# One unrolled plan for everything in front of the layers of a two-part transformer kernel

## The reference

```python
x = x + _layernorm(_L0_attn_ref(_layernorm(x), ...))
# inside, D = 128, H = 16 heads of 8, NB = 32 clusters a head, MLP = 512
x = _layernorm(inputs, ln1_g, ln1_b)
q = einsum('bsd,dhf->bshf', x, Wq); k, v likewise
qb = softmax(einsum('bshf,hfn->bshn', q, Whq)); kb likewise of k and Whk
logits = einsum('bqhf,bkhf->bhqk', q, k) / sqrt(8)
logits = logits + 0.1 * einsum('bqhn,bkhn->bhqk', qb, kb)
out = einsum('bhqk,bkhf->bqhf', softmax(logits), v)
x = einsum('bqhf,hfd->bqd', out, Wo) + inputs
y = _layernorm(x, ln2_g, ln2_b)
y = relu(y @ W1 + b1) @ W2 + b2
return x + y
```

## Time and profile before

| what | us |
| --- | --- |
| median of 3 runs | 3577.6 (3573.7 to 3582.4) |
| the profiled execution | 3577.4 |
| its span in the trace | 3575.6 |
| PE busy | 3290.2 (92%) |
| DVE busy | 2679.8 (75%) |
| ACT busy | 1740.4 (49%) |
| POOL busy | 1999.6 (56%) |

### The profile page before, as it was taken

How to read it: one execution, slowest core, us unless ns; L and a number is a source line. 1 busy time by engine, 2 the same in 40 slices (tenths; PEclk the granted TensorE clock), 3 DMA queues, 4 the chain that set the end, 5 groups by cost and what they waited for, 6 DMA issues and landing times. The chain is left out here.

```text
span 3575.6 us, 54667 instructions
## 1 busy us (share of the span) xinstructions
PE 3290.2 (92%) x17992; PEld 2168.8 (61%) x17992; DVE 2679.8 (75%) x4395; ACT 1740.4 (49%) x3293; POOL 1999.6 (56%) x1584
## 2 busy tenths in 40 slices
PE   5899989957999999999999999999999999999997
PEld 2455555435666666766666676666666766666676
DVE  7877877456787876778787677778786788878666
ACT  3276657633433446553434474443446654343464
POOL 2100000014777767676877656787867667787764
PEclk9588988977999999999999999999999999999999
DMA  0000000024223314632323154332324533232143
GB/s 16 0 2 2 1 1 1 1 62 103 57 63 72 72 25 148 174 82 60 72 63 71 43 173 131 72 72 66 69 48 123 162 98 70 59 72 63 34 157 117
DMA packets 139610, 248.15 MB, mean 69 GB/s; under 512 B 28416, under 2 KB 55936, under 8 KB 139072
## 3 DMA queue, kind: packets, MB, share of 16 engines
q1 hardware_dynamic: 139328, 244.64, 26.4%
HBM read 82.17 MB, written 27.53 MB: 31 GB/s over the span
## 5 line engine op out<-in xcount | busy, mean ns | idle before, releaser
L1128 ACT ACTIVATE prob<-psA 128x512 f32<-128x512 f32 x1152 | 652.7, 596 | 1048.1 <-PE psA L1440 459.2
L971 POOL TENSOR_TENSOR xw<-xw,prob 128x512 f32<-128x512 f32 x672 | 869.6, 1294 | 231.7 <-ACT prob L1128 157.1
L1707 DVE RECIPROCAL rden<-psO 128x256 f32<-128x256 f32 x256 | 448.6, 1753 | 134.4 <-PE psO L1471 131.5
L1439 PE MATMUL psA<-qs,ks 128*128 128x512 f32 x1152 | 524.8, 456 | 21.8 <-ACT prob L1128 17.7
L1733 DVE TENSOR_REDUCE mxp<-psA 128x1 f32<-128x512 f32 (+2 forms) x756 | 458.3, 662 | 43.6 <-PE psA L1416 29.1
L994 POOL TENSOR_TENSOR hidl<-gate,hidh 128x512 fp32r<-128x512 f32 x256 | 331.5, 1304 | 217.0 <-ACT hidh L1178 214.3
L1440 PE MATMUL psA<-qs,ks 128*128 128x512 f32 x1152 | 451.8, 392 | 0.0
L971 POOL TENSOR_TENSOR xw<-prob 128x512 f32<-128x512 f32 x224 | 288.5, 1288 | 286.4 <-ACT prob L1128 144.6
L1416 PE MATMUL psA<-ks,qs 128*128 128x512 f32 (+3 forms) x1344 | 409.4, 385 | 0.0
L1654 DVE TENSOR_REDUCE mxp<-psA 128x1 f32<-128x512 f32 x512 | 315.2, 682 | 40.4 <-PE psA L1254 40.4
L1051 ACT ACTIVATE pr<-psA 128x512 f32<-128x512 f32 x512 | 271.3, 599 | 125.9 <-PE psA L1265 124.6
(11 more groups left out here) (256 smaller groups left out, 6464.4 us busy)
## 6 DMA issues: line engine op xcount, KB each, us to landing
qs<-normed SPq DMA_DIRECT2D x256, 256.0 KB, 4.1
rbp<-rab SPq DMA_DIRECT2D x256, 192.0 KB, 3.4
spread<-routing_weights SPq DMA_DIRECT2D x128, 256.0 KB, 3.6
qs<-qs SPq DMA_DIRECT2D x64, 256.0 KB, 3.2
expert_weight_halves<-eh SPq DMA_DIRECT2D x32, 384.0 KB, 3.5
expert_weight_halves<-el SPq DMA_DIRECT2D x32, 384.0 KB, 4.3
eh<-expert_weight_halves SPq DMA_DIRECT2D x32, 384.0 KB, 3.2
el<-expert_weight_halves SPq DMA_DIRECT2D x32, 384.0 KB, 3.9
```

The source lines that it names most:

```text
L971: g.tensor_tensor(psum_k[:, t % 2, :], before, prob[:, i % 4, :], ALU.add).then_inc(s_su, 1 if kt > 1 else 2 + (t == 1))
L1128: act(prob[:, k % 4, :], psS[:, k % 2, :], ACT.Exp, scale=float(HD) ** -0.5).then_inc(s_ex, 1)
L1439: mm(psS[:, i % 2, :], ks[b][:, 0, tile], qs1[b][:, c, :, qs], start=True, stop=False)
L1707: vec.reciprocal(rden[:, :], psO[t % 2][:, 256:512]).then_inc(s_rd, 1)
```

## The change

Everything in front of the layers is put into one unrolled order, `opening_order`, planned once for all five engines and the DMAs:

- x is loaded in four chunks of four tiles. The norms are cut by chunk; the scaling by the reciprocal of the root moves to ScalarE (four instructions a chunk). Batch 0 goes first.
- q and k are projected directly in turned form, split once (`qkh`, `qkl`) and stored in DRAM (`qkd`); each stack's q and k rows are loaded from there.
- The cluster softmax is taken out of the front. Each pass does its own, for its four heads, in two halves of 1024 columns over two banks: 8 logit products, maximum, subtraction, exp, sum, reciprocal, product on GpSimd, 8 transposes, one high copy (ScalarE) and one low (VectorE).
- The stacks are filled by DMA from `thi` and `tlo`, with 24 transfers of 32 rows a pass, and nine from DRAM. There are three stacks in place of two.
- The maxima are taken over two banks at a time: 32 reductions of 1024 columns a pass. They go by half of the queries (c), each with a row of its own sent to the stack.
- PSUM is laid out anew: three banks for scores, one for the output, and two pairs of banks for everything else, which `planned` hands out (new arguments `ring` and `pairs`).
- The output of a pass is copied by ScalarE instead of VectorE. The tail (Wo, norm 2, MLP, norms 3 and 4) goes by chunk too, and batch 0's part may run beside the last pass. b2 is added on GpSimd.
- The hardware loop is gone.

```diff
-def planned(plan, priority, handover, late=0, narrow="", switch=0, slack=None):
+def planned(plan, priority, handover, late=0, narrow="", switch=0, slack=None, ring=None, pairs=0):
...
+    def vacant():
+
+        free_at = [(max([0] + [end[a] + handover for a in ring.get(holder, ())]), i) for i, holder in enumerate(held)
+                   if all(a in end for a in ring.get(holder, ()))]
+        return min(free_at) if free_at else (float("inf"), None)
...
+ROOTS = [(0, 0), (1, 0), (0, 1), (1, 1), (2, 0), (3, 0), (4, 0), (2, 1), (3, 1), (4, 1)]
+PASSES = NG1 * B
+STACKS = 3
+FILLS = 12
...
+    for p in range(PASSES):
+        g, b = divmod(p, B)
+        for s in range(2):
+            fill = ("land", ("TD", p, 0) if s else ("TD", p - 1, 1)) if s or p else None
+            stage("tensor", ("H", p, s), 1800, ("scalar", ("QC", 2 * b + 1)), ("tensor", ("T", p - 1, s)) if p else None)
+            banks(("H", p, s), ("vector", ("HS", p, s)))
+            stage("vector", ("HM", p, s), 1230, ("tensor", ("H", p, s)))
+            stage("vector", ("HS", p, s), 1230, ("vector", ("HM", p, s)))
+            stage("scalar", ("HE", p, s), 1150, ("vector", ("HS", p, s)))
+            stage("vector", ("HR", p, s), 1230, ("scalar", ("HE", p, s)))
+            stage("vector", ("HI", p, s), 250, ("vector", ("HR", p, s)))
+            stage("gpsimd", ("HN", p, s), 2700, ("vector", ("HI", p, s)))
+            stage("tensor", ("T", p, s), 1050, ("gpsimd", ("HN", p, s)), fill)
+            banks(("T", p, s), ("scalar", ("TH", p, s)), ("vector", ("TL", p, s)))
+            stage("scalar", ("TH", p, s), 1150, ("tensor", ("T", p, s)))
+            stage("vector", ("TL", p, s), 1250, ("scalar", ("TH", p, s)))
+            free = ("tensor", ("S", p - STACKS, N_S1 - 1)) if p >= STACKS else None
+            stored = ("land", ("QD", 3 if p else 1))
+            stage("sync", ("TQ", p, s), 3700 - 1800 * s, free, stored)
+            stage("sync", ("TD", p, s), 5000, ("scalar", ("TH", p, s)), free)
+            stage("sync", ("TE", p, s), 2500, ("vector", ("TL", p, s)), ("sync", ("TD", p, s)))
+            stage("land", ("TD", p, s), 3500, ("sync", ("TE", p, s)), ("sync", ("TQ", p, s)))
+        for c in range(2):
+            for t in range(4):
+                for h in range(HG):
+                    stage("tensor", ("M", p, c, t, h), 450, ("land", ("TD", p, 1)), ("tensor", ("J", p, 0)) if c and t + h > 1 else None)
+                    banks(("M", p, c, t, h), ("vector", ("M", p, c, t, h)))
+                    stage("vector", ("M", p, c, t, h), 1220, ("tensor", ("M", p, c, t, h)),
+                          ("tensor", ("J", p - 2, c)) if p > 1 else None)
...
+                stage("tensor", ("S", p, n), 225, ("land", ("JR", p, c)), ("scalar", ("S", *old)) if before > 2 else None,
+                      ("tensor", ("QT", 3)), ("tensor", ("VT", 3)))
+                used = divmod(p * 2 * TPB + j - 2, 2 * TPB)
+                stage("scalar", ("S", p, n), 603, ("tensor", ("S", p, n)), ("tensor", ("V", *used)) if p or j > 1 else None)
+            copied = divmod(2 * p + c - 1, 2)
+            stage("tensor", ("V", p, j), 740, ("scalar", ("S", p, j * HG + HG - 1)), ("gpsimd", ("F", p)),
+                  ("scalar", ("C", *copied)) if kt == 0 and (p or c) else None)
...
+OPENING, PAIR = opening_order()
...
-        psA = ctx.enter_context(nc.psum_tensor("psA", [P, 6, 512], F32))
-        psS, psM = psA[:, 0:4, :], psA[:, 4:6, :]
-        psO = [ctx.enter_context(nc.psum_tensor(f"psO{i}", [P, 512], F32)) for i in range(2)]
...
+        psA = ctx.enter_context(nc.psum_tensor("psA", [P, 8, 512], F32))
+        banks = [psA[:, i, :] for i in range(8)]
+        psS, psO = psA[:, 0:4, :], banks[6:8]
+        psS1, psO1 = psA[:, 0:3, :], banks[3]
...
+        def pair(*item):
+
+            i = PAIR[item][0]
+            return psA[:, 4 + 2 * i:6 + 2 * i, :].rearrange("p a n -> p (a n)")
...
+                elif what == "TD":
+                    p, s = i
+                    r = p % STACKS
+                    if p >= STACKS:
+                        sp.wait_ge(s_qk1, (p - STACKS + 1) * N_S1)
...
+                    sp.wait_ge(s_th, 2 * p + s + 1)
+                    for h in range(HG):
+                        for row in ((0, 64) if s else (0, 32)):
+                            put(s, r, row, h, thi[h * NB:(h + 1) * NB, :])
```

More of the change, by code:

```diff
@@ L93 @@
 STEPS = [(t, kt) for t in range(TPB) for kt in range(t + 1)]
-def planned(plan, priority, handover, late=0, narrow="", switch=0, slack=None):
+def planned(plan, priority, handover, late=0, narrow="", switch=0, slack=None, ring=None, pairs=0):
+    ring, held, taken = ring or {}, [None] * pairs, {}
     missing = {key: len(set(after)) for key, (_, after) in plan.items()}
@@ L118, in start @@
         turn = key[0] == "tensor" and (key[1][0] in narrow) != (before in narrow)
-        return max(ready[key], free.get(key[0], 0) + switch * turn)
+        return max(ready[key], free.get(key[0], 0) + switch * turn, vacant()[0] if key in ring else 0)
     chain, left = {}, {key: len(users.get(key, ())) for key in plan}
@@ L142, in planned @@
         key = choice()
-        end[key] = free[key[0]] = start(key) + plan[key][0]
+        began = start(key)
+        if key in ring:
+            i = vacant()[1]
+            taken[key[1]], held[i] = (i, held[i] and held[i][1]), key
+        end[key] = free[key[0]] = began + plan[key][0]
         del ready[key]
@@ L150, in planned, with rooted, chunked @@
     assert len(end) == len(plan)
-    return order
-def cluster_order(attend, prepare):
-    plan = {}
-    def stage(engine, name, cost, *after):
-        plan[engine, name] = (cost, [a for a in after if a])
-    if attend:
+    return (order, taken) if pairs else order
+ROOTS = [(0, 0), (1, 0), (0, 1), (1, 1), (2, 0), (3, 0), (4, 0), (2, 1), (3, 1), (4, 1)]
+PASSES = NG1 * B
+STACKS = 3
+FILLS = 12
+def rooted(k, b):
+    return ROOTS.index((k, b))
+def chunked(k, c):
+    return 2 * rooted(k, c // 2) + c % 2
@@ L528, in program @@
[L528 to L538 removed]
+        kst = [sb(f"kst_{i}", [P, HG, SEQ], F32R, where=first) for i in range(STACKS)]
@@ new lines, in program, with under @@
+        qst = [sb("qst_0", [P, 2, HG, 512], F32R, where=first)]
+        def under(name, shape, dt, *tiles):
+            below = ExitStack()
+            used = [sb(n, shp, d, where=below) for n, shp, d in tiles]
+            below.close()
+            return used, sb(name, shape, dt, where=first)
+        (xT, w_qkv), pr1 = under("pr1", [P, 2, HG, 512], F32, ("xT", [P, NT * P], F32), ("w_qkv", [P, 3, P], F32))
+        (qkl,), q = under("qst_1", [P, 2, HG, 512], F32R, ("qkl", [P, 2, NT * P], F32R))
@@ L724, in norm_vector @@
                 done(nc.vector.tensor_tensor(n.out[:, ts, :], x[:, ts, :], rstd[:, ts].unsqueeze(2).broadcast_to([P, 4, D]), ALU.mult))
-            def whole(c, dst):
-                v.wait_ge(n.ten, tbase + c + 1)
-                if bias is None:
-                    done(nc.vector.tensor_scalar(dst, psM[:, c % 2, :], gain, None, ALU.mult))
-                else:
-                    done(nc.vector.tensor_scalar(dst, psM[:, c % 2, :], gain, bias, ALU.mult, ALU.add))
-            if n.turned == "whole":
-                for c in range(4):
-                    whole(c, xT[:, c * 512:(c + 1) * 512])
         def norm_scalar(a, n, run=0, start=()):
```

1046 lines of the change are left out of this document (620 added, 426 removed).

## The result

The changed kernel takes 3438.0 us (median of 4 runs, 3433.1 to 3438.8), the kernel before 3580.0 in the same session: ratio 0.9601, 95% interval 0.9581 to 0.962. Forecast were 3380 and a range of 3325 to 3455. So the gain is 142 us where I had 197, and the question of the experiments is where the other 58 us went. (The profiled execution of the changed kernel took 3438.8, its span is 3437.0.)

What follows compares the result with a forecast made beforehand. TensorE and VectorE were taken as close to full inside a pass, with waits at its edges. Passes ending at 557, tail 31, 21 to the network and its 2768.9 gave 3378, with 1.8 around it 3380 us; range 3325 to 3455.

Steps and rivals of the forecast that it cites:

- rival A: Whole kernel: the forecast itself, TensorE at 0.92 in every pass, 3350 to 3415 us; chance 0.55.
- B: Passes: two pairs of banks are too few, VectorE waits at maxima for TensorE, 3415 to 3455 us; chance 0.22.
- Rival C: Stack fills: 32-row fills land in twice the time, 26 us a side, front loses 26 (3406); chance 0.07.
- step 1: Front: norms by chunk, softmax sides of pass 0 in turn, then maxima; first score at 92 us instead of 183.
- steps 2 and 4: Passes: TensorE needs 52.8 us a pass, at the 0.92 reached in full steps 57.4 us.
- step 2: Passes, TensorE: hardly relieved at 52.8 us a pass; three stacks remove the edge's 4 us wait and half clock.
- step 3: Passes, VectorE: 51 us a pass against 53.7 busy before; ScalarE 41, SP 21; none of VectorE, ScalarE, GpSimd bounds.
- step 5: Passes from 92 us: 443 of work, 10 for steps after the maxima, 12 for batch 0's tail; end at 557.
- step 6: Tail of batch 1: 31 us instead of 67; then 21 up to the first projection instead of 22.5.
- steps 6, 7: Behind the tail: 21 us up to the first projection, then the network untouched at 2768.9 us.
- Rival D: Whole kernel, better side: TensorE at 0.98 and first score at 80, 3325 us; chance 0.10 for 3325 to 3350.
- Rival E: Passes: waits on two bank pairs hold TensorE at its lower clock, ending near 900, about 3725 us; chance 0.04.

Runs made afterwards that it cites:

- experiment 6: Changed kernel with GpSimd's memset of the first stack moved behind norm 0's square sums, the two others behind the second cluster product; 3434.6 us, ratio 0.9578.
- experiment 1: Changed kernel with the nine q and k loads of each stack queued behind fills that are needed sooner; 3417.1 us, ratio 0.9527.
- experiment 4: Changed kernel with batch 0's tail made to wait for the last value product of the last pass; 3447.1 us, ratio 0.9613.
- experiment 3: Changed kernel with the second of the two products of each maximum left out, VectorE's work kept; 3414.3 us, ratio 0.9521.
- experiment 7, two stacks: Changed kernel with two stacks in place of three, the order planned anew; 3452.3 us, ratio 0.9628.
- half maxima: Changed kernel with row maxima taken over the first of the two banks only, all products kept; 3426.1 us, ratio 0.9554.
- planned costs: Changed kernel with a value product planned at 990 ns in place of 740, only the order changes; 3418.8 us, ratio 0.9535.
- the last kernel: Changed kernel with later loads behind fills (passes 2 to 7), a turned-cluster buffer per side, later zeroing and value products planned at 990 ns; 3401.5 us, ratio 0.9495.

## Why the prediction was right or wrong, step by step

The direction, the range and the place of the gain were right: 70 us in front, 45 in the passes, 28 in the tail. The likeliest time was 58 us too low, outside the range of rival A (3350 to 3415), in that of B, but not for B's reason: that the stated range of 3325 to 3455 held is owed to B's part of it, and so to luck: the largest single part of what was missing (26 us) came by C's mechanism, late fills and rows, to which I had given 0.07. Step by step:

- **Front (step 1), 92 forecast, 113 measured.** The chain was the one that I followed, one side behind the other because of the one buffer. Its terms were too small: the copies of the first projection end at 31.5 (25.5), 3.6 of these 6 us are the two means beside a memset (taking the memset away gave back 2.8, experiment 6); from there the q side's softmax takes 11.9 (10.5), its turn and copy 4.3 (2.1), the fills 13.9 (10.9), since they land behind the nine loads, and the k side 13.6 (13). So the first maxima product is at 75.3 and not at 62: 13 us of the 21. Of the rest the row is 9.9, 11.8 us in place of about 2, and the other terms 2 less than I gave them. I had counted the issues of the loads on SP's queue, but gave them no time on the DMA engines. Moving the loads in the front gave back only 4.3 of these 13 us (experiment 1).
- **Passes, TensorE's sum and its 0.92 (steps 2 and 4).** The size is right: without a load in the way and without the tail the eight passes would take 451.5 us (475.7 - 24.2, put together from experiments 1 and 4; no one kernel has both), and I had 443 + 10 = 453. That TensorE's work sets this pace is borne out in part: taking 7.4 us of it out of a pass gave 3.5 to 5.6 where no fill was late (experiment 3).
- **"Neither the 4 us wait nor the half clock behind it has a cause" (step 2).** This failed. The third stack does take the wait away that it is meant for (experiment 7), but the edges got another: fills and rows behind loads, 12.9 us in all. In the profile after, from 190 to 200, the granted clock is 0.83, behind the wait for the fills.
- **VectorE's 51 to 54 a pass is no bound (step 3).** Right, by half maxima (0.65 us a pass).
- **Last pass (step 5), 12 for batch 0's tail.** Mis-sized: 24.4. I had charged the table loads and let the products, 21.5 us of TensorE, lie in the gaps of the steps. They did not, or hardly.
- **Tail (step 6), 31 forecast, 39.6 measured.** The parts: turns and Wo 6.6 (4.7), norm 2 7.8 (4.6), turn with gain 2.2 (1.4), up- and down-products 16.4 (14.2), the rest 6.6 (6.3). The clock is 0.72 over the tail, 0.50 from 610 to 620: a short chain between engines leaves TensorE idle, and the up-products start at the lower level.
- **To the network, network (steps 6, 7).** 21.7 for 21; the network unchanged.
- **Rival C** named the late fills, but with the wrong size: it gave a side 26 us in the mean, through throughput. In fact most sides are on time, and a few are late because of what stands ahead: in the passes PE waited 3.1, 1.7 and 0.4 us for fills and 4.1 for a row. The sign that I had named for it, scores waiting for the row and the first maxima product for fills, is what the profile shows. (Its 26 is also too much by its own terms: the fills' 10.9 twice make a side of 13 one of 24.)
- **Rival D**'s 3325 does not follow from its terms: 0.98 takes 28 us off and a first score at 80 another 12, which is 3340.
- **Rival E** did not come: clock 0.98 in the passes.
- **The table load**, 1.28 us, or 2.66 with the drain for which the prediction cites the Trainium skill (ScalarE: Activation LUTs, "What ACT_TABLE_LOAD costs"). In the rows of experiment 4 the exp before ends at 556.86, the load begins at 556.88, takes 1.28, and the root begins at 558.17. There is no gap for a drain ahead of it or behind; the measurement decides, for the number that I took.

The miss of 59 us in the span is made of: loads ahead of fills and rows, 13 in the passes (what experiment 1 gave back) and 13 in front (3 of the fills, 10 of the row, by the lengths in the trace); batch 0's tail, 12; batch 1's tail, 9; the other terms of the front, 10; to the network and in it, 6, of which 5 are the spread of that stretch; less 4 charged too much. Still open: what holds up a row that has a queue to itself, what besides TensorE's work sets the pace of a pass, and how much of the gain of the planned costs comes from the banks.

## What to carry to other kernels

When a change moves work from the compute engines to DMAs, write down for each queue what stands ahead of every transfer that someone waits for, with its time on the DMA engines and not only its time of issue: a load for a pass that is far off can delay a fill that is needed at once, and it is free where the queue is idle. An overlap is worth what it saves behind less what it costs beside: a tail of 36.0 us, laid beside a pass of 47.0, made that pass 24.4 us longer. And if two edits each give 20 us, look in the trace whether they remove the same wait before adding them up.

## What the runs showed of the hardware

- Twelve fills of 128 KB, issued 0.64 us apart, land in 2.3 to 2.4 us each; behind nine loads of 8 rows (64 and 128 KB) such fills take 9.5 to 10.4, at a DMA share of 80% and 99 GB/s on average, where alone they moved 143 GB/s at 62.7%.
- A row of 8 KB lands in 1.8 to 2 us, also right behind eight fills (1.9, in the last kernel) or behind nine loads and twelve fills (1.8, two stacks); behind 18 loads and twelve fills it took 11.8, and 8.9 from ScalarE's queue, where nothing stood ahead.
- A VectorE step of 0.17 us on four columns a partition took 1.69 to 2.21 beside GpSimd's memsets, and 1.92 at 43.44 beside a GpSimd product of 1.91.
